# A graph network on one core: the variance with one tensor input, and the output's LayerNorm beside layer 2's group

## What is computed

```
def layer(h, wl, b_l, ws, b_s, wr, b_r, g, beta):
    u = einsum('bid,bjd->bij', h, h) / sqrt(D)
    delta = softmax(u) * adjacency
    attn = delta / (delta.sum(-1) + 1e-10)
    hl, hs, hr = h @ wl.T + b_l, h @ ws.T + b_s, h @ wr.T + b_r
    ctx = (attn * upper) @ hl + diagonal(attn) * hs + (attn * lower) @ hr
    o = (ctx - mean(ctx)) / sqrt(var(ctx) + 1e-12) * g + beta
    return relu(o)
y = x + layer2(layer1(x))
out = (y - mean(y)) / sqrt(var(y) + 1e-5)
```

## Time and profile before

| | |
|---|---|
| three timed runs | 1751.63, 1752.2, 1754.78 us; median 1752.2 |
| span of the profiled execution | 1751.1 us, first to last instruction |
| mean granted clock of TensorE | 0.994 |
| busy: TensorE, its weight load | 1700.1 us (97%), 1649.2 us (94%) |
| busy: VectorE, POOL, ScalarE | 1549.8 us (89%), 1383.5 us (79%), 960.6 us (55%) |
| DMA engines | 18% busy, 56 GB/s |

### The profile page before, as it was taken

The page is one execution under the profiler, slowest core; times in us unless marked ns, Lnnn a source line. Parts: engine busy times, 40 slices in busy tenths (PEclk is TensorE's granted clock), DMA queues, the critical chain, the costliest instruction groups (busy, mean ns, idle before and its releaser), DMA issues.

```text
span 1751.1 us, 34427 instructions
## 1 busy us (share of the span) xinstructions
PE 1700.1 (97%) x10112; PEld 1649.2 (94%) x10112; DVE 1549.8 (89%) x4122; ACT 960.6 (55%) x2310; POOL 1383.5 (79%) x1930
## 2 busy tenths in 40 slices
PE   7999999999999999999999999999999999999995
PEld 7999999999999999999999999999999999999995
DVE  6888988888988898888889888989898989888996
ACT  5555555555555555555555555555555555555553
POOL 3787888887888778887888787888788887888885
PEclk9999999999999999999999999999999999999997
DMA  4121111111111111121112111211111111111111
GB/s 162 46 60 49 55 52 57 51 54 54 55 55 49 56 53 55 49 60 49 55 49 60 49 55 50 60 51 54 54 56 53 52 57 53 55 49 59 50 45 38
DMA packets 93904, 97.62 MB, mean 56 GB/s; under 512 B 10688, under 2 KB 92864, under 8 KB 93888
## 3 DMA queue, kind: packets, MB, share of 16 engines
q1 hardware_dynamic: 93888, 97.43, 18.2%
HBM read 72.22 MB, written 25.17 MB: 56 GB/s over the span
## 4 chain that ended last, share of the span: by engine, by line
DVE 38%; POOL 29%; issue 21%; ACT 9%; PE 2%; DVEq 1%; POOLq 1%; DMA 0%; ACTq 0%; SPq 0%
DVE veps L453 13%; POOL rstd L688 9%; DVE y L431 7%; POOL shifted L228 7%; POOL scaled L224 7%; DVE stats L436 7%; ACT normed L602 5%; ACT p_score L585 3%; DVE gathered L423 3%; POOL nbias L691 3%; DVE moments L442 2%; DVE neg_mean L456 2%; PE p_proj L322 2%; DVE moments L445 1%; POOL attnT_split L682 1%
## 5 line engine op out<-in xcount | busy, mean ns | idle before, releaser
L322 PE MATMUL p_proj<-w,hT_layer 128*128 128x384 f32 x6912 | 1409.2, 345 | 0.6 <-DVE w L500 0.6
L322 PEld LDWEIGHTS p_proj<-w,hT_layer 128*128 128x128 f32 x6912 | 1155.6, 189 | 9.3 <-DVE w L500 1.0
L602 ACT ACTIVATE normed<-gathered,nbias,rstd 128x384 f32<-128x384 f32 x256 | 181.4, 709 | 722.1 <-POOL nbias L691 722.1
L218 POOL TENSOR_TENSOR proj_split<-proj,proj_split 128x768 fp32r<-128x768 f32 x252 | 464.1, 1842 | 5.3 <-issue 5.3
L453 DVE SCALAR_TENSOR_TENSOR veps<-eps_units,moments 128x1 f32<-128x1 f32 (+1 forms) x259 | 330.6, 1276 | 21.4
L377 PE MATMUL p_gather<-proj_split,attnT_split 128*128 128x384 f32 x1536 | 310.9, 337 | 9.0 <-DVE proj_split L218 3.5
L682 POOL TENSOR_TENSOR attnT_split<-attnT,attnT_split 128x256 fp32r<-128x256 f32 x256 | 189.8, 741 | 126.5 <-DVE rows L485 123.1
L377 PEld LDWEIGHTS p_gather<-proj_split,attnT_split 128*128 128x128 f32 x1536 | 271.8, 189 | 9.6 <-issue 7.3
L466 DVE TENSOR_TENSOR proj<-p_proj,bias_all 128x768 f32<-128x768 f32 x256 | 241.5, 943 | 4.6 <-PE p_proj L322 4.6
L316 PE MATMUL p_score<-hT_layer 128*128 128x256 f32 x768 | 216.0, 283 | 5.0 <-POOL hT_layer L707 5.0
L596 ACT ACTIVATE proj_split<-proj 128x768 fp32r<-128x768 f32 x256 | 212.7, 831 | 0.0
(11 more groups left out here) (47 smaller groups left out, 1630.8 us busy)
## 6 DMA issues: line engine op xcount, KB each, us to landing
xt_raw<-xT SPq DMA_DIRECT2D x128, 192.0 KB, 2.4
xn<-x SPq DMA_DIRECT2D x128, 192.0 KB, 2.5
out<-o SPq DMA_DIRECT2D x128, 192.0 KB, 1.9
adj_layer<-adj SPq DMA_DIRECT2D x256, 64.0 KB, 1.9
w_raw<-WT SPq DMA_DIRECT2D x6, 576.0 KB, 7.5
bias_all<-bias SPq DMA_DIRECT2D x2, 576.0 KB, 9.1
gain<-gain_row SPq DMA_DIRECT2D x1, 192.0 KB, 9.5
shift<-shift_row SPq DMA_DIRECT2D x1, 192.0 KB, 10.6
```

Source lines behind the costliest of these rows:

```text
L218: op.tensor_tensor(proj_split[k][:, LO], proj[k][:, UP:LOW + 1, :], proj_split[k][:, HI].bitcast(F32), ALU.subtract).then_inc(s_proj_lo[k], 1)
L322: return nc.tensor.matmul(p_proj[:, which, 0:D], hT[k][:, slot, st, c, :], w[:, k, which, mv, c, :], start=(n == 0), stop=(n == 8))
L602: nc.scalar.activation(rows_out, rows_in, ACT.Identity, bias=nbias[k][:, which:which + 1], scale=rstd[k][:, which:which + 1]).then_inc(s_r ...
```

## The change

The variance of a layer becomes a `tensor_scalar`: one tensor (`eps_units`), a constant, and `moments` as a pointer scalar, one value per partition. The output's variance is `moments` plus a constant; the second column of `eps_units`, which held its epsilon, goes, and with it the two memsets of the setup. `normalise_rows` is split into functions for a layer and for the output. The output's functions are called behind layer 2's mask and ahead of layer 2's own group; on ScalarE the output `o` follows layer 2's `normed`; on POOL the power on two numbers is now layer 2's and the output's (`both_deviations`), and layer 1's is on one. Where there is no layer 2 beside it, the output's group stands where it stood.

```
-                nc.vector.scalar_tensor_tensor(
-                    out=veps[k][:, which], in0=eps_units[k][:, slot, which], scalar=GNN_EPS,
-                    in1=moments[k][:, which, 1], op0=ALU.mult, op1=ALU.add)
-                nc.vector.tensor_scalar(neg_mean[k][:, which], moments[k][:, which, 0], -1.0, None,
-                                        ALU.mult).then_inc(last, 1)
+            def row_variance(k, b, slot, s_last):
+                done(dve, s_moments[k], b)
+                done(dve, s_denom2[k], b)
+                nc.vector.tensor_scalar(veps[k][:, LAYER:LAYER + 1], eps_units[k][:, slot:slot + 1], GNN_EPS,
+                                        moments[k][:, LAYER, 1:2], ALU.mult, ALU.add)
+                nc.vector.tensor_scalar(neg_mean[k][:, LAYER:LAYER + 1], moments[k][:, LAYER, 0:1], -1.0, None,
+                                        ALU.mult).then_inc(s_last, 1)
+            def output_moments(b, slot):
+                done(dve, s_shifted, b)
+                moved(dve, s_xn, b, slot)
+                done(dve, s_o, b - 1)
+                nc.vector.scalar_tensor_tensor(out=y[:], in0=shifted[:], scalar=0.0,
+                                               in1=xn[:, slot, :], op0=ALU.max,
+                                               op1=ALU.add).then_inc(s_y, 1)
+                done(dve, s_y, b)
+                nc.vector.bn_stats(stats6[:, 2], y[:]).then_inc(s_y_stats, 1)
+                done_apart(dve, s_y_stats, b)
+                nc.vector.bn_aggr(moments[1][:, FINAL], stats6[:, 2]).then_inc(s_y_moments, 1)
+            def output_variance(b):
+                done(dve, s_y_moments, b)
+                nc.vector.tensor_scalar(veps[1][:, FINAL:FINAL + 1], moments[1][:, FINAL, 1:2], OUT_EPS, None,
+                                        ALU.add)
+                nc.vector.tensor_scalar(neg_mean[1][:, FINAL:FINAL + 1], moments[1][:, FINAL, 0:1], -1.0, None,
+                                        ALU.mult).then_inc(s_y_veps, 1)
...
-                if live(i, i - 1) or live(i, i - 4):
-                    normalise_rows(0, i - 1 if live(i, i - 1) else None, q,
-                                   i - 4 if live(i, i - 4) else None, p)
+                if live(i, i - 1):
+                    normalise_layer1(i, q)
+                if live(i, i - 4) and not live(i, i - 2):
+                    normalise_output(i, p)
...
+                if live(i, i - 4) and live(i, i - 2):
+                    normalise_output(i, p)
                 if live(i, i - 3) and not last_graph(i) and not after_last_graph(i):
-                    normalise_rows(1, i - 3, q, None, 0)
+                    normalise_layer2(i, q)
...
                 if live(i, i - 3) and not last_graph(i) and not after_last_graph(i):
                     normalise(1, i - 3, s_nbias[1], LAYER, gathered[1][:], normed[1][:], s_normed[1])
+                    if live(i, i - 4):
+                        finish(i, p)
...
+            def both_deviations(b, b_y):
+                done(pool, s_y_veps, b_y)
+                done(pool, s_veps[1], b)
+                nc.gpsimd.tensor_tensor(rstd[1][:], veps[1][:], neg_half[:], ALU.pow).then_inc(s_rstd[1], 1)
+                done(pool, s_rstd[1], b)
+                nc.gpsimd.tensor_tensor(nbias[1][:], neg_mean[1][:], rstd[1][:],
+                                        ALU.mult).then_inc(s_nbias[1], 1)
```

More of the change, by code:

```diff
@@ L104, in graph_block @@
         normed = [sb(f"normed{k}", [P, D]) for k in (1, 2)]
-        stats6 = [sb(f"stats6_{k}", [P, 2, 6]) for k in (1, 2)]
+        stats6 = sb("stats6", [P, 3, 6])
         rows = [sb(f"rows{k}", [P, 2, COLS]) for k in (1, 2)]
@@ L114, in graph_block @@
         neg_mean = [sb(f"neg_mean{k}", [P, 2]) for k in (1, 2)]
-        eps_units = [sb(f"eps_units{k}", [P, 2, 2]) for k in (1, 2)]
+        eps_units = [sb(f"eps_units{k}", [P, 2]) for k in (1, 2)]
         veps = [sb(f"veps{k}", [P, 2]) for k in (1, 2)]
@@ new lines, in row_moments @@
+            def row_moments(k, b, slot):
+                done(dve, s_gather[k], b)
+                done(dve, s_diag[k], b)
+                if k == 1:
+                    done(dve, s_normed[k], b - 1)
+                nc.vector.scalar_tensor_tensor(
+                    out=gathered[k][:], in0=proj[k][:, SELF, :], scalar=col(rows[k], slot, DIAG),
+                    in1=p_gather[k][:, 0:D], op0=ALU.mult, op1=ALU.add).then_inc(s_whole[k], 1)
+                done(dve, s_whole[k], b)
+                nc.vector.bn_stats(stats6[:, k], gathered[k][:]).then_inc(s_stats[k], 1)
+                done_apart(dve, s_stats[k], b)
+                nc.vector.bn_aggr(moments[k][:, LAYER], stats6[:, k]).then_inc(s_moments[k], 1)
@@ L603, in normalise, with finish @@
                                      scale=rstd[k][:, which:which + 1]).then_inc(s_rows, 1)
+            def finish(i, p):
+                moved(act, s_out, i - 6, p)
+                beside = live(i, i - 2)
+                normalise(1, i - 3 if beside else i - G - 2, s_nbias[1] if beside else s_y_nbias, FINAL, y[:],
+                          o[:, p, :], s_o)
             def high_input(b, slot):
@@ L637, in iteration @@
                     normalise(1, i - 3, s_nbias[1], LAYER, gathered[1][:], normed[1][:], s_normed[1])
-                if live(i, i - 4):
-                    moved(act, s_out, i - 6, p)
-                    beside = live(i, i - 1)
-                    normalise(0, i - 1 if beside else i - G - 1, s_nbias[0] if beside else s_y_nbias, FINAL,
-                              y[:], o[:, p, :], s_o)
+                if live(i, i - 4) and not live(i, i - 2):
+                    finish(i, p)
                 if live(i, i + 1):
@@ L732, in iteration @@
                 if after_last_graph(i):
[L733 removed]
+                    deviation(1, i - 3)
                 if live(i, i - 1):
[L737 to L740 removed]
+                    deviation(0, i - 1)
+                if live(i, i - 4) and not live(i, i - 2):
+                    output_deviation(i - 4)
                 if live(i, i + 1):
```

89 lines of the change are left out of this document (33 added, 56 removed).

## The result

| kernel | timed runs | median | range |
|---|---|---|---|
| before | 4 | 1752.91 us | 1751.63 to 1754.78 |
| after | 4 | 1712.13 us | 1709.17 to 1712.51 |

The ratio is 0.9764 (95% interval 0.975 to 0.9778): the change takes 41 us off, 2.4%. The forecast was 1703 with a range of 1697 to 1756, so the direction was right and the gain was forecast 9 us, or a fifth, too large. The profiled execution after has a span of 1710.8 us (before 1751.1) at a granted clock of 0.993.

What follows compares the result with a forecast made beforehand. POOL's queue was taken as the bound, TensorE waiting. Chain 13.30 + 0.25 - 0.16 + 0.16 - 0.33 - 0.17 - 0.16 = 12.89, plus 0.13 for loop ends; taken as 13.03, 49.6 us off over 124 graphs: 1703 us, range 1697 to 1756.

Steps and rivals of the forecast that it cites:

- The bound: In the loop, POOL's queue sets the 13.30 us turn and TensorE waits for it; TensorE alone would need 13.00.
- `y` holds L682: Layer 2's half: `y` starts 0.16 ahead of POOL's L682, which must wait for it: +0.25 a turn, bounds 0 and 0.55.
- the other case: Rival: L682 starts before `y`, which waits; VectorE is late for layer 2's power; chain 13.62, 1792 us; chance 0.10.
- The form is free: Variance as `tensor_scalar` with one tensor and a pointer no longer waits for L218: 0.33 a turn off, bounds 0 and 0.33.
- The first rival: The new variance form is held by POOL too: chain 13.22, 1742 us; chance 0.22, plus 0.06 with a bad branch.
- VectorE is in time by 0.12: Layer 2's half: variance and `neg_mean` done at 828.84, before L218 ends at 828.96.
- the term -0.16: Layer 2's half: with the variance not held, the power follows L218 directly, 1.84 behind its start instead of 2.00.
- Layer 1's L218 to the power: Layer 1's half: with the variance not held, the power follows L218 directly, 1.84 instead of 2.01 behind its start: -0.17.
- L699: Layer 1's half: POOL's L699 is no longer held by `y`; L699 to L218 goes from 0.82 to 0.49: -0.33.
- both widths: On POOL, the power on one number in layer 1's half gives -0.16, on two in layer 2's half +0.16.
- the largest gain of 53 us: Whole loop: the most the rows allow, 0.43 a turn for 124 graphs, given as 1698.
- Within 1 us: Start and end of the program: setup loses two memsets, the end keeps its stages; effect within 1 us.

Runs made afterwards that it cites:

- the kernel with the late `y`: The changed kernel with four unread one-number VectorE instructions ahead of `y`, so that POOL starts first: 1806.34 us, ratio 1.0299.
- the form alone: The kernel before with only the new variance form; the output's group stays beside layer 1's: 1719.26 us, ratio 0.9812.
- the kernel with `y` ahead of the mask: The changed kernel with `y` issued ahead of layer 2's mask, its statistics and variance still behind it: 1700.0 us, ratio 0.9699.
- the kernel with the three unread instructions: The changed kernel with three unread `tensor_scalar` of 2, 8 and 384 numbers behind layer 1's `neg_mean`: 1741.04 us in one run.
- the same with single numbers: The kernel before with the new variance form and `neg_mean` as two one-number instructions: 1704.05 us, ratio 0.9711.
- the last kernel: The changed kernel with `y` ahead of layer 2's mask and the last graph's iteration's output group placed as before: 1699.23 us, ratio 0.9688.
- the move alone: The changed kernel with its layer variances back on two tensors; the output's group stays beside layer 2: 1731.31 us, ratio 0.9875.

## Why the prediction was right, and what was off

**The bound: right.** POOL's chain set the turn and TensorE waited. With every hindrance gone TensorE's turn is 12.97 (forecast 13.00), and no version came below it.

**`y` holds L682: right in size.** +0.25 forecast, +0.25 measured. That it starts ahead of POOL was the condition, and the kernel with the late `y` shows the price of the other case: 13.69 without loop ends where the rival said 13.62.

**The form is free: right for one number, and only so.** The first rival is refuted for this change by the 126 variances that begin under L217 and take 0.21 us, but its mechanism is real for two and more numbers. This was in part luck. I took the 0.33 because the form is nearest to `gathered` with its pointer, and that reason doesn't carry it: a `tensor_scalar` on 2, 8 or 384 numbers is held, and none of these has a pointer. What decided was that the variance has one number, which stood only as a weak argument against the rival (155 ns against 141). That hint fits, but it is faint: one-number instructions differ as much among themselves (the output's variance takes 154 ns in after and 144 in the form alone). With `neg_mean` on two numbers the gain is smaller, as the form alone shows.

**"VectorE is in time by 0.12": this step failed.** The power starts 1.91 behind L217 in layer 2's half, and not the 1.80 that layer 1's half and the kernel with `y` ahead of the mask have. The row at 835.56 shows it: `neg_mean` ends at 835.70, when L217 is about to end at 835.79, and the power starts 0.15 behind `neg_mean`. I asked whether VectorE ends before L217 does; it must end some 0.1 earlier, since the power would otherwise start before L217's row ends (842.96 against 843.01 in layer 1's half). And the variance with a pointer takes 0.21 where I took the 0.16 of the earlier trace rows. This is the term -0.16 that came out as -0.09. The kernel with `y` ahead of the mask bears it out: `neg_mean` ends there 1.41 behind L217's start on average, in place of 1.77, and the power is back at 1.80.

**The small terms.** Layer 1's L218 to the power gave -0.21 where -0.17 was said, L699 -0.30 for -0.33, both widths as said. The chain was forecast as 12.89 and is 12.92; with the loop's ends it is 13.05, not 13.03. One slip changed nothing: the largest gain of 53 us was given as 1698, which is the span; the time would be 1699.

**Start and end: a mis-sized term.** "Within 1 us" was said. 124 turns at 0.36 are 45 us, the span fell by 40.3. The timeline of TensorE finds most of the difference. At the start of after, the second nine projections and the transposes that answer to the earlier trace rows:

```profile
10.83 3.25 PE L321 MATMUL p_proj<-w,hT_layer 128*128 128x384 f32 x9 [0.94 <-DVE w L510]
...
49.13 0.49 PE L398 MATMUL p_gather<-ident,normed 128*128 128x128 f32 x3
```

They stand 2.0 us later than in the earlier trace rows, and 1.4 of it is this one group of projections, which takes 1.86 before (at 10.30). That is not the change's: across the twelve traces of this study the same transposes stand between 46.94 and 49.13, and in the kernel with the three unread instructions, whose setup is that of after, at 47.07. It goes with TensorE's granted clock. The trace's record of it begins with the full clock (2.4 GHz) at 9.3 us before and at 14.9 after, the latest of the twelve. Nine projections ahead of that point take 3.0 to 3.3 us in both, and nine behind it 1.8 to 1.9; the nine at 13.94, across it, take 2.26 in after where before's next nine take 1.81. So the group at 10.83 ran at the lower of the two levels, which is inferred from its time, since the record holds nothing ahead of 14.9. At the end, the last two gathers of after:

```profile
1690.43 1.23 PE L376 MATMUL p_gather<-proj_split,attnT_split 128*128 128x384 f32 x6
1697.58 2.15 PE L376 MATMUL p_gather<-proj_split,attnT_split 128*128 128x384 f32 x6 [4.07 <-DVE proj_split L217]
```

They are 7.15 apart, 6.07 before, and this is the change's: it is 7.1 to 7.4 in every kernel with after's order at the end, 6.13 in the three with before's (the form alone, the same with single numbers, and the last kernel) and 6.5 to 6.6 with `y` ahead of the mask. The last gather waits for VectorE's split of the projections, and the output's group now stands ahead of it. From the last gather to the end of the span after takes 13.2 and before 12.3, and most of this is the clock again. The gather takes 2.15 in after, where the granted clock falls to 0.5 (1.2 GHz) 0.12 behind its start. Before, the clock falls 1.04 behind its start:

```profile
1738.76 1.37 PE L377 MATMUL p_gather<-proj_split,attnT_split 128*128 128x384 f32 x6 [2.88 <-DVE proj_split L218]
```

Where it has fallen before the gather begins, as in eight of the twelve traces, the gather takes 2.26 and the rest 13.2 to 13.8. In both kernels TensorE stands before this gather, for 2.88 us before and 4.07 after. 2.0 at the start and 2.0 at the end leave some 0.7 unassigned. I had not followed the written-out iterations at the end one by one, and had taken the start of a single execution as fixed.

**Why the whole is less than its parts.** The form alone gives 33, the move alone 21, both 41. In layer 1's half each removes the same hold of the variance by L218, the one by its form and the other by coming earlier: from L218 to the power the form alone takes off 0.07, the move alone 0.22, both 0.21. In layer 2's half the form alone takes off 0.20 and the move alone adds 0.07, but both take off 0.09 and not 0.13, since the move makes VectorE late there. Together that is some 0.11 a turn, or 14 us for 124 turns; 33 and 21 have 13 over 41.

## What to carry to other kernels

Where VectorE and POOL run side by side, look for instructions whose end coincides with one of POOL's: they are held, and the cure can be as small as one number per instruction instead of two, or issuing VectorE's large instruction ahead of the event that starts POOL. Before counting on such a repair, ask which engine is the bound after it: here the same form was worth 33 us and then nothing. And when an instruction is said to be in time, compare it with the moment at which the next one starts where nothing holds it, not with the end of the one in front.

## What the runs showed of the hardware

- A `tensor_scalar` in fp32 from SBUF to SBUF on one number per partition runs beside a POOL instruction in 0.14 to 0.21 us; on two or eight it lasts until POOL's ends (1.83 us). One on 384 numbers that starts 0.03 us ahead makes POOL's the longer one (2.03 for 1.84).
- A one-number `tensor_scalar` with a pointer and two operations takes 214 ns (L430), one with a constant and one operation 144 to 154. The second operation is not likely the cause, since the old variance, two operations on two tensors with a constant, took 0.16 alone; the pointer was not tested by itself.
- `y` (two SBUF tensors, 0.56 alone) begun 0.16 ahead of a POOL instruction makes that one 0.99 in place of 0.74; begun 0.08 behind it, `y` itself takes 1.07.
- With a loop body of eight graphs VectorE stands for 2.8 us in 14 of 15 passes, each time around the start of an 8 KB packet of the instruction queue, which has 83 packets in place of 10. A body of four has no such stall and no such packet in its passes between 107 and 1635 us.
